# A decoder block in float32 on one core: affine norms evicted once, mixtures and value sums from SBUF, low-rank stage by halves of tokens, new orders on every engine

## The reference, cut to what matters

```
x = x + rwkv(layernorm(x));  x = x + head_mix(layernorm(x), ctx);  x = x + low_rank(layernorm(x))

rwkv(x):  h = layernorm(x)*ln1_w + ln1_b;  hh = h one token earlier (0 before the first)
          xk, xv, xr = h*m + hh*(1-m)            # three shares m per feature
          k = xk Wk^T; v = xv Wv^T; sr = sigmoid(xr Wr^T)
          rwkv = sr * scan(k, v)                 # exact recurrence over the 256 tokens, per feature
          x = x + rwkv Wo^T
          h = layernorm(x)*ln2_w + ln2_b;  xk, xr = h*m + hh*(1-m)
          return x + sigmoid(xr Wrec^T) * (relu(xk Wkey^T)^2 Wval^T)       # 256 -> 1024 -> 256
head_mix: per token: 16 heads of 16 features; scores head x head, masked to the lower triangle,
          softmax, weighted sum of the heads of ctx
low_rank: gelu(x U1 V1 + b1) U2 V2 + b2          # 256 -> 64 -> 1024 -> 64 -> 256
```

## Time and profile before

| | us |
|---|---|
| runs | 1204.00, 1201.18, 1203.92 (median 1203.92) |
| span of the profiled execution | 1199.4 |
| its own time | the page gives only the span |
| PE busy | 1020.8 (85%) |
| DVE busy | 952.5 (79%) |
| ACT busy | 940.2 (78%) |
| POOL busy | 901.1 (75%) |
| mean granted clock of PE | 0.947 |

### The profile page before, as it was taken

The page is one execution under the profiler, slowest core; times in us unless marked ns, Lnnn a source line. Parts: engine busy times, 40 slices in busy tenths (PEclk is TensorE's granted clock), DMA queues, the critical chain, the costliest instruction groups (busy, mean ns, idle before and its releaser), DMA issues.

```text
span 1199.4 us, 14602 instructions
## 1 busy us (share of the span) xinstructions
PE 1020.8 (85%) x3584; PEld 586.0 (49%) x3584; DVE 952.5 (79%) x2092; ACT 940.2 (78%) x2007; POOL 901.1 (75%) x862
## 2 busy tenths in 40 slices
PE   2569698989899898989899898989898998969506
PEld 1237264654647363655646373645546473727202
DVE  3654889898989899798979898898979888757470
ACT  3778779888888979888888889888888888584504
POOL 0220997969696988969696978969696969978780
PEclk9889799999999999999999999999999999989767
DMA  5010020201111020201111110202011010201000
GB/s 176 18 23 31 1 53 1 71 0 54 18 54 19 9 62 1 72 0 53 18 53 18 33 38 1 72 0 62 9 53 36 17 37 0 54 1 36 1 17 18
DMA packets 38983, 38.54 MB, mean 32 GB/s; under 512 B 2932, under 2 KB 38648, under 8 KB 38904
## 3 DMA queue, kind: packets, MB, share of 16 engines
q1 hardware_dynamic: 30456, 29.38, 7.4%
q0 software_dynamic: 8448, 8.39, 4.6%
HBM read 29.38 MB, written 8.39 MB: 31 GB/s over the span
## 4 chain that ended last, share of the span: by engine, by line
PE 46%; ACT 25%; DVE 13%; issue 7%; POOL 6%; SPq 1%; DMA 0%; ACTq 0%; POOLq 0%; DVEq 0%
PE bank L832 18%; PE bank L889 12%; PE bank L920 5%; ACT n L480 4%; PE bank L839 4%; DVE bank L1345 4%; POOL prod L329 3%; ACT shift L473 3%; ACT q L480 3%; PE bank L913 3%; PE bank L932 2%; POOL prod L350 2%; DVE stat L1154 2%; ACT hidden L598 1%; ACT rr L546 1%
## 5 line engine op out<-in xcount | busy, mean ns | idle before, releaser
L329 POOL TENSOR_TENSOR prod<-q,kv_ctx 128x256 f32<-128x256 f32 (+5 forms) x448 | 360.1, 853 | 140.6 <-ACT q L480 140.6
L350 POOL TENSOR_TENSOR prod<-prob,v_dh 128x256 f32<-128x256 f32 (+3 forms) x256 | 383.9, 1606 | 0.0
L832 PE MATMUL bank<-xk,w_key 128*128 128x512 f32 x512 | 233.4, 605 | 11.3 <-DVE xk L1196 11.3
L889 PE MATMUL bank<-w_val,hidden 128*128 128x256 f32 x1024 | 225.9, 379 | 0.0
L1345 DVE TENSOR_REDUCE bank<-prod 128x64 f32<-128x256 f32 (+3 forms) x256 | 192.0, 819 | 34.8 <-POOL prod L350 25.4
L889 PEld LDWEIGHTS bank<-w_val,hidden 128*128 128x128 f32 x1024 | 193.5, 190 | 31.7 <-issue 6.7
L1318 DVE TENSOR_REDUCE score<-prod 128x16 f32<-128x256 f32 (+5 forms) x448 | 177.1, 466 | 19.5 <-POOL prod L329 19.4
L832 PEld LDWEIGHTS bank<-xk,w_key 128*128 128x128 f32 x512 | 97.7, 193 | 127.7 <-issue 111.0
L846 PE MATMUL bank<-ident,n 128*128 128x128 f32 x384 | 66.2, 302 | 103.4 <-ACT n L480 101.0
L565 ACT ACTIVATE hidden<-bank 128x512 f32<-128x512 f32 x128 | 74.1, 593 | 82.8 <-PE bank L832 82.7
L846 PEld LDWEIGHTS bank<-ident,n 128*128 128x128 f32 x384 | 49.3, 155 | 159.6 <-issue 153.7
(11 more groups left out here) (95 smaller groups left out, 1909.9 us busy)
## 6 DMA issues: line engine op xcount, KB each, us to landing
x_in<-in_x SPq DMA_DIRECT2D x16, 512.0 KB, 3.5
x<-in_x POOLq DMA_DIRECT2D x16, 512.0 KB, 5.7
kv_ctx<-in_ctx SPq DMA_DIRECT2D x16, 512.0 KB, 4.5
out<-y_out SPq DMA_DIRECT2D x16, 512.0 KB, 3.2
w_key<-in_wkey SPq DMA_DIRECT2D x1, 1024.0 KB
w_val<-in_wval SPq DMA_DIRECT2D x1, 1024.0 KB
w_k<-in_wk SPq DMA_DIRECT2D x1, 256.0 KB, 3.6
w_v<-in_wv SPq DMA_DIRECT2D x1, 256.0 KB, 4.4
```

Of the source, the lines that this page charges most:

```text
L329: ins = pool.tensor_tensor(o, a, b, ALU.mult)
L350: ins = pool.tensor_tensor(o, ph[:, HB * n:HB * n + HB, 0:keys].unsqueeze(2).to_broadcast(shape), vh[:, :, 0:keys].unsqueeze(1).to_broadca ...
L832: mm = pe.matmul(to[:, :], w[:, fi, P * f:P * f + P], src[:, fi, :], start=(fi == 0), stop=(fi == CH - 1))
L889: mm = pe.matmul(bank[6 + t // 2][:, C * (t % 2):C * (t % 2) + C], hidden[:, j, P * t:P * t + P], w_val[:, j, :], start=(j == 0), stop=(j ...
```

## The change

- Norm 1 and norm 2: ACT evicts each transposed tile once, with weight and bias, into a new SBUF tile `h1` or `h2` with a zero column before each sequence (`affine_1`, `affine_2`). The own share is an ACT instruction from there (`own_share`), and DVE's `add_before` reads the shifted `h`, with `other` = 1 - m as its scalar. The one-column instructions and the combined coefficients are gone.
- The shift of every norm is one DVE instruction of four columns; the negated mean is gone. `scale_back` is one exponent of four columns, of a difference that DVE makes in `shift_1`.
- Value sums go to an SBUF tile `o_sum`, where they are divided and from which x3 is made. `last_residual` writes into x3, which is stored; `y_out` is gone, `n4` shares the buffer of `n2`.
- Low-rank stage by halves of tokens: the two halves of 256 tokens lie in the two halves of the partitions from U1 to V2. Gelu reads both halves from two banks with one instruction.
- Banks: every product has banks of its own choice (`K_BANK`, `V_BANK`, ...). All orders are new. The last projection, residual and store of a group move to lag 5 (steps run to 20), the transposes of norm 1 to lag 0, SP's load of x to two groups ahead, at the end of its step.

```diff
-            def now_part(dst, f, src, name, norm):
-                ...
-                act.activation(out[:, :, 0:1], x[:, :, 0:1], ACT.Identity,
-                               bias=first_b[:, m, f:f + 1], scale=w)
-                return act.activation(out[:, :, 1:T], x[:, :, 1:T], ACT.Identity,
-                                      bias=col(norm + "_b", f), scale=w)
+            def affine_1(g, f):
+                act.wait_ge(tr1_mm, upto(g, 2, f + 1))
+                ...
+                act.activation(now(h1, f), by_seq(TR1_BANK[f]), ACT.Identity,
+                               bias=col("ln1_b", f), scale=col("ln1_w", f)).then_inc(h1_done, 1)
+            def own_share(dst, f, src, name):
+                return act.activation(seqs(dst, f), now(src, f), ACT.Identity, scale=col(name, f))
             def add_before(dst, f, src, name):
-                x = src[:, :].rearrange("p (s t) -> p s t", s=SEQ)
-                out = seqs(dst, f)[:, :, 1:T]
-                return dve.scalar_tensor_tensor(out=out, in0=x[:, :, 0:T - 1], scalar=prev_w[:, m, f:f + 1],
+                out = seqs(dst, f)
+                return dve.scalar_tensor_tensor(out=out, in0=before(src, f), scalar=other[:, at:at + 1],
                                                 in1=out, op0=ALU.mult, op1=ALU.add)
-            def shift_of(n, g):      # ACT
-                for t in range(TT):
-                    ins = act.activation(shift[n][:, t:t + 1], nmean[n][:, t:t + 1], ACT.Identity,
-                                         scale=rstd[n][:, t:t + 1])
+            def shift_of(n, g, done):      # DVE
+                dve.wait_ge(rstd_done[n], upto(g, 1))
+                if some(g):
+                    dve.wait_ge(done, upto(g - 1, 1))
+                return dve.scalar_tensor_tensor(out=shift[n][:, :], in0=mv[n][:, :, 0], scalar=-1.0,
+                                                in1=rstd[n][:, :], op0=ALU.mult, op1=ALU.mult)
+                dve.tensor_tensor(ln_ratio[:, :], lnc[:, :], lnv[1][:, :], ALU.subtract)   # in shift_1
-                    ins = dve.tensor_reduce(bank[5][:, row:row + HB * HD], src, AX.X, ALU.add)
+                    ins = dve.tensor_reduce(o_sum[:, row:row + HB * HD], src, AX.X, ALU.add)
-                o = bank[5][:, :].rearrange("p (h d) -> p h d", d=HD)
+                o = o_sum[:, :].rearrange("p (h d) -> p h d", d=HD)
-                dve.tensor_tensor(pair(x3[par], s), bank[5][:, :], pair(x2[par], s), ALU.add)
+                dve.tensor_tensor(pair(x3[par], s), o_sum[:, :], pair(x2[par], s), ALU.add)
             def project_u1(g):
                 for fi in range(CH):
-                    mm = pe.matmul(bank[3][:, :], w_u1[:, fi, :], n4T[:, fi, :],
+                    for e in range(2):
+                        mm = pe.matmul(bank[U1_BANK][RANK * e:RANK * e + RANK, 0:W // 2], w_u1[:, fi, :],
+                                       n4T[:, fi, W // 2 * e:W // 2 * e + W // 2],
                                        start=(fi == 0), stop=(fi == CH - 1))
             def project_v1(g, jj):
-                    pe.matmul(bank[HIDDEN_BANKS[j % 4]][:, :], w_v1[r:r + RANK, j // 2, :],
-                              pT[r:r + RANK, :], start=True, stop=True).then_inc(v1_mm, 1)
+                    for e, to in ((0, LOW_BANK[jj]), (1, HIGH_BANK[jj])):
+                        rows = slice(RANK * e, RANK * e + RANK)
+                        mm = pe.matmul(bank[to][:, at:at + W // 2], w_v1[rows, j, :], pT[rows, :],
+                                       start=True, stop=True)
...
```

On ACT the normalisation of norm 3 follows directly on its exponent (`rstd_of`), and `normalise_1` stands among the gelus:

```diff
+                if on(3):
+                    use_table(EXP_SET)
+                    rstd_of(3, i - 3)
+                    normalise_3(i - 3, 1 - p)
+                if on(4):
+                    use_table(EXP_SET)
+                    variance_ln(4, i - 4)
...
```

More of the change, by code:

```diff
@@ new lines, in affine_2, with ffn_own_k @@
+            def affine_2(g, f):
+                act.wait_ge(tr2_mm, upto(g, 2, f + 1))
+                if some(g):
+                    act.wait_ge(xk2_done, upto(g - 1, 2, f + 1))
+                    act.wait_ge(xr2_done, upto(g - 1, 2, f + 1))
+                act.activation(now(h2, f), by_seq(TR2_BANK[f]), ACT.Identity,
+                               bias=col("ln2_b", f), scale=col("ln2_w", f)).then_inc(h2_done, 1)
+            def ffn_own_k(g, f):
+                act.wait_ge(h2_done, upto(g, 2, f + 1))
+                own_share(xk, f, h2, "ffn_tmk").then_inc(gk_done, 1)
@@ L541, in exp_e1 @@
                 act.wait_ge(split_done, upto(g, 2, f + 1))
-                act.activation(bank[f][:, :], bank[f][:, :], ACT.Exp, scale=-1.0).then_inc(e1_exp, 1)
+                act.activation(bank[K_BANK[f]], bank[K_BANK[f]], ACT.Exp, scale=-1.0).then_inc(e1_exp, 1)
             def exp_bonus(g, f):
@@ L585, in copy_n4T @@
                 act.wait_ge(tr4_mm, upto(g, 2, f + 1))
-                if f == 0 and some(g):
+                if some(g):
                     act.wait_ge(u1_mm, upto(g - 1, 1))
-                act.activation(n4T[:, f, :], bank[4][:, :], ACT.Copy).then_inc(n4T_done, 1)
+                act.activation(n4T[:, f, :], bank[TR4_BANK[f]], ACT.Copy).then_inc(n4T_done, 1)
             def copy_pT(g):
@@ L850, in transpose_1 @@
                 pe.wait_ge(n1_done, upto(g, 1))
-                transposes(bank[2 + f], f, n1[par], tr1_mm)
+                transposes(bank[TR1_BANK[f]], f, n1[par], tr1_mm)
             def project_k(g, f):
```

1293 lines of the change are left out of this document (782 added, 511 removed).

## The result

The changed kernel takes 1357.08 us (median of 4 runs, 1353.83 to 1361.15), the kernel before beside it 1202.55 (1200.25 to 1204.00): ratio 1.129, interval 1.127 to 1.132. The forecast was 1233, its range ended at 1285. The sign was right, and so was the kind of cause, waits of DVE for POOL; the size of the rise, 154 us and not 29, was not, and the failed step is the bound on one such wait.

The account below looks back on a forecast made before the run. A ring of dependences between engines, none of them full, bounds the step. Twelve steps x (69.5 - 66.8) = +32.4, drain -3, on the 1199.4 span give 1228.8; with 4.5 to the median, 1233; range 1135 to 1285.

Parts of the forecast that it names:

- the failed step: DVE instructions with two SBUF inputs beside POOL: each waits between nothing and one whole POOL instruction, at most 2.44 us.
- The ring without waits: Steady step's loop of dependences between engines, without DVE's waits for POOL: DVE's load 59.8 us plus 1 allowed for idling.
- rival 1: Two SBUF inputs on DVE cost nothing and the step shrinks to 62 us: 1143, from 1120 to 1180; chance 0.35.
- The turns: DVE and POOL exclude each other instruction by instruction: 14 DVE waits of 0.63 us, 8.8 us a step.
- POOL pays 12 x 0.7 = 8.4: POOL also waits for DVE's two-input instructions: 8.4 us a step, so its load becomes 64.6 us, which fits.
- PE -1.7 a step: Low-rank stage on PE: first and last product by halves go from 1.73 to about 0.87 us each.
- Shifts over DVE: 0 a norm: Norms' shifts moved from ACT to DVE: bounds -0.85 to +1.5 us for one norm, 0 taken.
- Twelve steps, start 0, drain -3: Whole run: twelve steps x (69.5 - 66.8) = +32.4 us, nothing at the start, some 3 us saved in the drain.
- the forecast step of 69.5: Steady step after the change: DVE's load 68.6 us with waits, plus 1 allowed for idling, against 66.8 before.
- Rival 2: POOL alone pays, stopping under each of DVE's 14 wide instructions: a step of 67.5 us, 1210; chance 0.12.
- Rivals 3 and 4: Nothing paid or won, 1204 us, chance 0.09; PE's low-rank halves don't overlap, +1.7 us a step, 1 in 20 within others.
- the signs named: New profile: DVE's mixes average 1.0 to 1.5 us, spread to 3; DVE over 95% busy, ACT under 80%; first low-rank product 0.9.

Follow-up runs that it names:

- the first study: No kernel around it: POOL rows of 8 to 24 products, one DVE instruction started behind the k-th; two SBUF inputs behind k = 8 and 11 waited short.

## Why the prediction was wrong, step by step

- **The ring without waits.** DVE's own load 59.8 plus 1, or 62 in rival 1: the step without second inputs is 61.2, or some 61.7 with mixes of full length. Right. Against the kernel before, the order, the halves and the shorter ACT part are worth 95 us by themselves (1202.6 to 1107.5); of the parts tried alone, the halves make 9 of it and the shifts' move is a loss. What the order and the evictions give one by one was not tried.
- **The turns.** 14 waits of 0.63 us, 8.8 a step. Measured where nothing else is left: 139.8 us over 16 groups, 8.7 a step, of which the ten mixes make 5.7 at 0.57 each; in the changed kernel itself the waits up to 2.5 us make 7.9. Right, and by the assumed mechanism. (The step should read 69.6: 59.8 + 8.8 + 1.)
- **The failed step: "The price lies between nothing and a wait for the whole POOL instruction in flight, at most 2.44 us."** That upper bound was no bound. It assumed that the waiting engine comes next. The runs showed that it does not once POOL has issued 15 instructions since its last stop or turn, or its DMA since its last stop: 18 waits of up to 11.8 us, 135.2 us in all, 8.5 a step. 61.2 + 7.9 + 8.5 is 77.6, the measured mean interval 77.2. The range, built on that bound, ended at 1285.
- **Where the shut rows came from.** Both parts of the cause were in the profile of before, which I read for durations only: POOL's DMA stands in the middle of its step, and POOL ran 24 and then 28 instructions, the DMA counted, between two idle stretches, in nearly every step (a count from its records in order of time).
- **POOL pays 12 x 0.7 = 8.4.** Its busy time rose by 4.3 a step (56.2 to 60.5). While it shuts DVE out it pays nothing: the eight value products of the row shown took 12.24 us, and 12.8 by the means of the earlier trace rows.
- **PE -1.7 a step.** -0.9 by itself. The first low-rank product takes 1.08 us, not 0.9, and the time gained 0.5 a step. Which wait took the rest was not followed up.
- **Shifts over DVE: 0 a norm**, between -0.85 and +1.5. +0.2 measured, in the form of four instructions.
- **Twelve steps, start 0, drain -3.** There are 15 intervals, and the start became 13.1 us shorter, the drain 1.5 longer. 15 x 10.9 - 13.1 + 1.5 is the 152 us of the spans. With the forecast step of 69.5 the same terms give 1199.4 + 15 x 3.2 - 11.6, some 1236, beside the 1228.8 of the sum: by luck the counting errors nearly cancel.
- **The rivals.** Rival 1 is what one-input copies come near to: 1143 against 1107.5. Rival 2 is out: DVE paid most. Rivals 3 and 4 are out too: the two inputs cost 250 us, and the halves do overlap. Of the signs named, DVE over 95% of its step and ACT under 80% came true. The mixes' mean of "1.0 to 1.5 us" and their spread "up to 3 us" did not: 1.8 in the mean over all ten, and up to 9.2.

The forecast with the failed step taken out has a kernel to stand beside: the changed one without shut rows runs at 1252.9, 20 us above 1233 and inside the range. Its 61.2 + 8.7 is 69.9, the measured mean interval 70.3.

## What to carry to other kernels

Before an operand of a DVE instruction is moved from PSUM to SBUF, list what POOL runs beside it, and count POOL's instructions between two real stops, not only their length: here the wait was the rest of one instruction in a short row and the whole rest of a long one. Where such an instruction must stay, let POOL wait for its own last result every few instructions, and keep its DMAs right ahead of a place where it stands still in any case. And when a wait is removed or moved, ask who inherits the row: taking away 172 us of waits at the mixes gave back 72.

## What the runs showed of the hardware that I had not expected

- At 512 columns the border lies between 14 and 15 POOL instructions, the same in both repeats (1.73 and 6.61 us). At 256 columns it lies between 11 (1.19 us) and 16 (5.95 us).
- A DVE instruction of four columns pays the same wait as one of 512 (1.20 against 0.15 us), and one of a single column with a scalar column none (0.20 us in 256 cases). One of 512 columns with a scalar column took 1.47 us beside a row; what it takes alone was not measured, so its wait is not shown.
- Four instructions with two SBUF inputs a step cost 175 us in one order, 21 with one stop more.
- After POOL's DMA the next products' records overlap by 0.5 us and are longer by as much (1.75 against 1.26 us), until POOL stops; in a trace that marks a row shut by the DMA. A row shut by the count has no such mark (1.26 us in the 24 products of the first study).
